# Context keys and values projected between the expert tiles and the narrow attention; all 24 shared units in front of the tiles

## What is computed

```python
x = x + moe(layernorm(x))        # 16 experts, 4 a token, plus a shared expert
# self attention of layer 1, 16 heads of 16 channels ("narrow")
q, k = rms(rms(x) @ Wq + bq), rms(rms(x) @ Wk + bk)
x = x + softmax(q k^T / 4) v @ Wo + bo
# cross attention of layer 1: 16 query heads, 4 key/value heads of 128
q = rmsnorm(x @ Wq + bq, qn_w)                 # x: layernorm of the residual
k = rmsnorm(ctx @ Wk + bk, kn_w)               # ctx: an input, 16 x 128 x 256
v = ctx @ Wv + bv
x = x + (softmax(q k^T / sqrt(128) + mask) v) @ Wo
x = x + bitlinear_ffn(layernorm(x))
```

## Time and profile before

| | us |
|---|---|
| median of 3 runs | 1897.95 |
| lowest, highest | 1893.75, 1899.11 |
| profiled execution | 1894.33 (span 1892.5) |
| granted TensorE clock, mean | 0.934 of full |
| PE busy | 1639.5 (87%) |
| DVE, ACT, POOL busy | 1256.6 (66%), 877.7 (46%), 549.8 (29%) |
| DMA | 143.37 MB, 76 GB/s in the mean |

### The profile page before, as it was taken

How to read it: one execution, slowest core, us unless ns; L and a number is a source line. 1 busy time by engine, 2 the same in 40 slices (tenths; PEclk the granted TensorE clock), 3 DMA queues, 4 the chain that set the end, 5 groups by cost and what they waited for, 6 DMA issues and landing times. The chain is left out here.

```text
span 1892.5 us, 25681 instructions
## 1 busy us (share of the span) xinstructions
PE 1639.5 (87%) x8566; PEld 1307.3 (69%) x8566; DVE 1256.6 (66%) x2677; ACT 877.7 (46%) x2528; POOL 549.8 (29%) x443
## 2 busy tenths in 40 slices
PE   6999979988997877799997688799878999999866
PEld 5878868776876655577775366577657887788644
DVE  4654786777688666454445556765656778877878
ACT  4534434434443444122222334555336666666666
POOL 2132331723352163300005654552123122211000
PEclk9999999988999898899998678899899999999989
DMA  7243433422352062233334110000100111000001
GB/s 262 68 137 120 160 99 112 169 95 95 130 190 98 28 178 68 73 106 106 107 93 141 34 34 23 23 1 1 45 24 28 39 41 41 12 1 1 1 1 45
DMA packets 82072, 143.37 MB, mean 76 GB/s; under 512 B 8981, under 2 KB 44437, under 8 KB 81813
## 3 DMA queue, kind: packets, MB, share of 16 engines
q1 hardware_dynamic: 75796, 124.94, 20.3%
q0 software_dynamic: 6144, 16.79, 2.7%
HBM read 86.90 MB, written 54.79 MB: 75 GB/s over the span
## 5 line engine op out<-in xcount | busy, mean ns | idle before, releaser
L2308 ACT ACTIVATE self_attention<-self_attention,small 128x128 f32<-128x128 f32 x256 | 99.9, 392 | 121.8 <-DVE small L1634 121.8
L2838 POOL TENSOR_TENSOR cross_attention_heads<-cross_attention_heads 128x512 f32<-128x512 f32 x64 | 70.4, 1100 | 285.2 <-DVE cross_attention_heads L1977 285.2
L2453 ACT ACTIVATE narrow_attention<-bank,small 128x128 f32<-128x128 f32 x256 | 90.4, 365 | 110.7 <-DVE small L1867 110.4
L759 PE MATMUL bank<-self_attention 128*128 128x256 f32 x512 | 130.4, 400 | 12.8 <-DVE residual L1653 12.8
L2537 ACT ACTIVATE cross_attention_heads<-cross_attention_heads,small 128x128 f32<-128x128 f32 x256 | 99.6, 390 | 90.2 <-DVE small L2001 90.2
L1103 PE MATMUL bank<-cross_attention,cross_attention_heads 128*128 128x256 f32 x512 | 124.8, 387 | 15.0 <-DVE residual L2015 10.1
L2704 POOL DMA_INDIRECT narrow_attention<-picked_outputs,dispatch x64 | 62.8, 981 | 235.4 <-DMA picked_outputs<-tiles 207.4
L563 PE MATMUL bank<-x_channel_major,qkv_weights_split 128*128 128x512 f32 x256 | 118.0, 461 | 6.6 <-DVE qkv_weights_split L1671 2.9
L759 PEld LDWEIGHTS bank<-self_attention 128*128 128x128 f32 x512 | 101.0, 201 | 32.3 <-DVE residual L1653 16.4
L1103 PEld LDWEIGHTS bank<-cross_attention,cross_attention_heads 128*128 128x128 f32 x512 | 95.5, 191 | 38.3 <-DVE residual L2015 22.3
L2640 POOL CAST qkv_weights_split<-self_attention 128x1024 fp32r<-128x1024 f32 x45 | 49.5, 1100 | 249.2 <-DMA self_attention<-in_wqkv 195.0
(11 more groups left out here) (382 smaller groups left out, 4735.6 us busy)
## 6 DMA issues: line engine op xcount, KB each, us to landing
picked_inputs<-self_attention SPq DMA_DIRECT2D x64, 512.0 KB, 6.2
self_attention<-in_wqkv SPq DMA_DIRECT2D x48, 512.0 KB, 6.1
experts_far<-picked_inputs SPq DMA_DIRECT2D x79, 128.0 KB, 2.0
picked_outputs<-tiles SPq DMA_DIRECT2D x79, 128.0 KB, 1.7
self_attention<-in_wo SPq DMA_DIRECT2D x16, 512.0 KB, 4.1
experts<-in_moe SPq DMA_DIRECT2D x4, 1408.0 KB, 13.8
self_attention<-in_bv SPq DMA_DIRECT2D x16, 256.0 KB, 5.3
bitnet_weights<-in_bitgu SPq DMA_DIRECT2D x8, 416.0 KB, 3.3
```

The lines of the kernel that those rows point to most:

```text
L759: m = T.matmul(bank[7][:, 0:D], ZT_a[n % 2][:, h, :], wo_a[p % 2][:, h, :], start=h == 0, stop=h == HG - 1)
L2308: m = S.activation(P_a[u][:, h, :], P_a[u][:, h, :], ACT.Exp, bias=negmax_a[u][:, h:h + 1], accum_out=sums_a[u][:, h:h + 1])
L2453: m = S.activation(n_P[v][:, h, :], s4_in[:, h, :], ACT.Exp, bias=n_negmax[v][:, h:h + 1], accum_out=n_sums[bb % 2][:, q4 * 4 + h:q4 * 4 + ...
L2838: G.tensor_tensor(x_qsq, x_queries[f % 2], x_queries[f % 2], ALU.mult).then_inc(x_squared, 1)
```

## The change

- **Shared units.** All 24 units stand in front of the tiles (`NUNIT` in place of `NBEFORE` in the loops of all four engines). The tiles of PE wait for `e_added` of all four groups.
- **Loads and splits during the tiles.** At tiles 4 to 7 SP loads the context weights in four pieces of 256 KB, at 8 the biases, at 10 to 13 and 34 to 37 ctx in eight pieces. ACT makes the high parts of ctx at four steps of the tile loop (20, 24, 46, 50). POOL, which did nothing in the tiles, splits the context weights and makes the low parts of ctx. DVE's share of the ctx split (L1951) and POOL's `context_weights` in the narrow steps are gone.
- **Between tiles and narrow attention.** PE runs `keys_of(bb)` and `values_of(bb)` for the 16 batches. The turns of group 0's norm stand behind batches 9 and 10, the projections of the narrow attention behind 11 and 12. DVE adds the key bias (16 key tiles are kept) and does the four combines, the moments and the norm between them. ACT copies the values without bias; SP stores each batch's values to DRAM (`kept_v`, 16 x 256 KB).
- **In the narrow steps.** ACT squares the keys of one batch at each odd step 5 to 35, DVE sums them a step later; two roots (24, 40) and two inverses (25, 41), POOL scales the keys at steps 26 to 40 (even) and 42 to 49, PE and ACT turn them at steps 48 to 63. The norms of groups 0 to 2 for the cross attention stand at steps 49 to 62. POOL splits the first query weights at step 53.
- **Behind it.** There is no context stage. The lead of the cross attention follows `n_added(B)` with the norm of the last group beside it. SP loads the kept values (4 x 1 MB), then the mask and the second query weights. `weigh` becomes an activation that adds the value bias.
- The SBUF layout changes so that the 16 key tiles live through the narrow attention.

The core of the diff:

```diff
-NBEFORE = NUNIT - NSH
+KEY_SQUARE = {5 + 2 * c: c for c in range(B)}
+KEY_NORM = {(26 + 2 * c if c < B // 2 else 42 + c - B // 2): c for c in range(B)}
+KEY_ROOT, KEY_INVERSE = {24: 0, 40: 1}, {25: 0, 41: 1}
+KEY_TURN = {48 + c: c for c in range(B)}
+CROSS_MOMENTS = {49 + 4 * g: g for g in range(NG - 1)}
+CROSS_NORM = {50 + 4 * g: g for g in range(NG - 1)}
+CROSS_TURN = {51 + 4 * g + 2 * kt: (g, kt) for g in range(NG - 1) for kt in range(KT)}
...
# PE
-            for i in range(NBEFORE + LAG):
-                if i < NBEFORE:
+            for i in range(NUNIT + LAG):
+                if i < NUNIT:
...
-            pe.wait_ge(e_added, KT * (NG - 1))
+            pe.wait_ge(e_added, KT * NG)
...
             pe.wait_ge(t_outs, NTILE)
-            for i in range(NBEFORE, NUNIT + LAG):
...
+            for bb in range(B):
+                keys_of(bb)
+                values_of(bb)
+                if bb in (9, 10):
+                    turn_xt(NORM["second", 0], bb - 9)
+                if bb in (11, 12):
+                    narrow_project(2 * (bb - 11))
+                    narrow_project(2 * (bb - 11) + 1)
             for b in range(GB):
                 narrow_heads(b)
...
+                    if n in KEY_TURN:
+                        turn_keys(KEY_TURN[n])
+                    if n in CROSS_TURN:
+                        turn_xt(NORM["cross", CROSS_TURN[n][0]], CROSS_TURN[n][1])
...
-            for bb in range(B):
-                side.step()
-                keys(bb)
-                side.step()
-                cross_values(bb)
...
+            pe.wait_ge(n_added, B)
             turn_bias(0)
+            side.add(second_norm(NG - 1, "cross"))
             for f in range(LEAD):
                 x_filled(f)
...
# ACT
+                    if n in KEY_SQUARE:
+                        square_keys(KEY_SQUARE[n])
...
-                S.copy(ZT_x[n % 2], four(bank[6][:, :])).then_inc(x_Z.sem, 1)
+                hg = n // (GB * NG)
+                S.activation(ZT_x[n % 2], four(bank[6][:, :]), ACT.Identity, bias=v_bias[:, hg:hg + 1]).then_inc(x_Z.sem, 1)
...
# POOL
+                    if n in KEY_NORM:
+                        scale_keys(KEY_NORM[n])
+                    if n == 53:
+                        pool.wait_ge(combined, TOPK * B)
+                        split_wq(0)
...
# SP
+            for bb in range(B):
+                sp.wait_ge(c_v, bb + 1)
+                D_(kept_v[bb * P:(bb + 1) * P, :], v_out_c[bb % 2]).then_inc(v_stored[bb % 2].sem, 16)
+            sp.wait_ge(n_proj, 2 * B)
+            fetch_wq(0)
...
             sp.wait_ge(n_added, B)
             for g in range(NG):
+                D_(x_v[:, g * GB:(g + 1) * GB, :], kept_v[g * GT:(g + 1) * GT, :].rearrange("(b p) c -> p b c", p=P)).then_inc(got_v[g].sem, 16)
             D_(x_mask, io["mask"]).then_inc(got_mask, 16)
             fetch_wq(1)
```

460 lines of the change are left out of this document (228 added, 232 removed).

## The result

| | before | after |
|---|---|---|
| median, us | 1895.97 (4 runs, 1893.75 to 1899.11) | 1881.65 (4 runs, 1880.33 to 1888.95) |
| profiled execution, span | 1892.5 | 1887.1 |

The ratio is 0.9932, with a 95% interval of 0.9912 to 0.9952: 9 to 17 us faster, where 35 were forecast. The time, 1881.65, lies inside the range that was given, but only in the part that was added for the dear case; the main case was 1850 to 1878.

A forecast was written before the change was run, and what follows sets the result against it. PE was taken to bound the tiles, shared units and last narrow steps. 19 + 0 - 3 + 32.5 - 85.4 + 1.5 + 1.6 = -33.8 from 1894.33 gave 1860.5, set halfway at 1863; range 1844 to 1884.

The forecast's parts named there:

- dear case: Rival, steps 48 to 63: ACT and PE alternate at being last, each turn costs a whole wait; 1887 us; chance 0.15.
- main case: Whole kernel: the forecast as worked out, 1863 us, 1850 to 1878 with the terms' own ends; chance 0.53.
- A: Start of the tiles: six more units ahead fill a 10.5 us PE hole; first tile 19 us later.
- B: The tiles: added context loads, ACT copies and POOL splits cost 0 us (0 to +3).
- C: Last tile to first narrow score: PE runs context batches and projections without a break; -3 us (-5 to +4).
- D: Narrow attention steps: added squares, sums, roots, key turns and three norms cost +32.5 us (+18 to +50).
- slower rival: Inserted groups open gaps, PE's clock drops, steps 16 to 63 keep the first stretch's pace; 1922 us; chance 0.05.
- E: Last narrow sum to first cross score: context stage gone, -85.4 us; returning values add +1.5.
- F: Cross attention: 64 copies become activations adding the value bias; +1.6 us (0 to +7.9).
- Late values: Rival: value loads and mask share engines with other loads, cross attention opens 12 us late; 1875 us; chance 0.09.
- cheap steps: Rival, narrow steps: the chain hides the squares and full PE keeps the clock up; 15 us, 1845; chance 0.15.

## Why the prediction was wrong, point by point

- **A, held.** +19.7 and +20.0 against +19. The units filled the hole; the wait behind them is 2.63 for DVE's sums.
- **B, held.** The tiles took 1.2 us less.
- **C, nearly.** -1.0 and -0.7 on the maxima, 0 on the first score, against -3 with ends at -5 and +4. PE ran through as worked out, with one wait of 3.9 that was denied ("Nothing breaks this row"); the tail was inside its bounds.
- **D, squares and sums: held.** +10.6 and +7.7 over steps 0 to 47 against 9.5.
- **D, key turns: mis-sized a little.** 9.9 in place of 7.0.
- **D, norms: the step that failed.** "Three such places come, in steps 49 to 58, where half a load more is uncovered: 3 x 4.3 = 13", with 2.7 for the turns. Measured 32. The 3.70 of the earlier trace rows was taken as the price of a norm. It is PE's wait in one norm, and three things were not in it. The order: there ACT takes the root in the step of the moments, and it was ready when DVE came to it; here ACT takes it a step later, in the step of the normalisation and behind that step's exponentials and key copy, so DVE waited 3.76 each time with the next maximum queued behind it. Moving the normalisation later gave back 17, some of it by meeting less of POOL's work and by the clock. POOL beside the normalisation, which doubled or quadrupled it at two of three places. And the clock: behind each gap PE ran 8 to 12 us at the lower level; filling the gaps gave back 5.5, all of it behind two of the three norms. These parts overlap and can't be added.
- The trace of before had shown the last one (1.10 and 2.05 around the same wait): the forecast itself named the lower clock as the slower rival, but priced it for all 48 steps or not at all.
- **Slips that decided nothing.** The terms of D add up to 32.2 and its lower end to some 15.5, where 32.5 and 18 stand. The row at 1149.00 is the root's, not an exponential's; the exponential behind the second load starts as soon after it in that trace (1149.32 + 1.28, then 1150.61).
- **The bound "ACT 48.2, PE 49.0", misleading.** Busy sums say how long the stretch must be at least. They say nothing on an order that makes both wait.
- **E, held.** -84.3 and -85.7 against -83.9, the values' return included. 285 GB/s in the stretch, faster than the 268 that was used, and no block of queries waited for it.
- **F, held.** +1.8 and +0.7 against +1.6.
- **The rivals.** "Dear steps" had the right place and nearly the right size (D at 56, measured 50 to 53), but another mechanism: the norms and not the turns. That the time lies inside the range is owed to this rival's price, and is luck as far as the mechanism goes. Late values, cheap steps, the pace of the first stretch in all later steps did not happen.
- The sum with the measured D, 50 to 53 in place of 32.5, is -16 to -13. The runs gave -14.3.

## What to carry to other kernels

When work is put into the steps of a coupled pipeline, write down for each inserted instruction that waits what stands behind it in the same engine's order and who waits for that; leave as many steps between the halves of a chain that crosses engines as the chain is long, and look in which step each engine does its part. The price of one place in a trace holds only where the order around it is the same. A stage at 100% on one engine says that inserted work of this engine is paid, and nothing on what a wait there costs. And see what the queue that is never late (here POOL) will be doing at the chosen place, since an engine that runs ahead of the steps does not do its work at the step where the code puts it.
